# Spreading the attention denominators as high and low rows, and two reciprocals one expert unit earlier

## The reference

```python
q, k = relu(qkv[..., :8]), relu(qkv[..., 8:16]); v1 = concat([v, ones])
kv  = einsum('bgnd,bgne->bgde', k, v1)          # 32 heads of 8 channels
out = einsum('bgnd,bgde->bgne', q, kv)
out = out[..., :8] / (out[..., 8:] + EPS)       # numerators / denominators
x = x + batchnorm(conv1x1(out, w_proj))
t = (x - mean) / sqrt(var + 1e-5)               # norm over channels
probs = softmax(t @ router); keep the top 2 of 8
x = x + t + sum_e combine_e * (gelu(t @ w1[e] + b1[e]) @ w2[e] + b2[e])
```

## Time and profile before

| | us |
|---|---|
| median of three runs | 3474.5 |
| lowest and highest | 3469.59, 3474.97 |
| the profiled execution, its own time | 3470.55 |
| its span, first to last instruction | 3468.8 |
| TensorE busy | 3045.2 (88%) |
| VectorE busy | 1727.8 (50%) |
| ScalarE busy | 1512.8 (44%) |
| GpSimd busy | 853.9 (25%) |

### The profile page before, as it was taken

How to read it: one execution, slowest core, us unless ns; L and a number is a source line. 1 busy time by engine, 2 the same in 40 slices (tenths; PEclk the granted TensorE clock), 3 DMA queues, 4 the chain that set the end, 5 groups by cost and what they waited for, 6 DMA issues and landing times. The chain is left out here.

```text
span 3468.8 us, 66009 instructions
## 1 busy us (share of the span) xinstructions
PE 3045.2 (88%) x26432; PEld 1701.1 (49%) x26432; DVE 1727.8 (50%) x2317; ACT 1512.8 (44%) x2263; POOL 853.9 (25%) x694
## 2 busy tenths in 40 slices
PE   6766683899999975999998769999999999999989
PEld 1166321455555532566666234646454554646455
DVE  6724286577766440111111254656465555555575
ACT  4412351567677751111222344535454554545434
POOL 3500350344444421111110103121221213121322
PEclk7668675999999985999999789999999999999999
DMA  4611675123433324677777344655645564646244
GB/s 178 237 25 24 217 282 205 67 109 146 155 146 150 150 116 130 186 214 213 208 212 243 113 155 149 208 168 175 205 166 196 164 213 141 234 146 226 100 149 161
DMA packets 233863, 579.59 MB, mean 167 GB/s; under 512 B 38444, under 2 KB 105260, under 8 KB 225068
## 3 DMA queue, kind: packets, MB, share of 16 engines
q1 hardware_dynamic: 233684, 577.26, 49.8%
HBM read 384.24 MB, written 192.94 MB: 166 GB/s over the span
## 5 line engine op out<-in xcount | busy, mean ns | idle before, releaser
L2137 DVE TENSOR_TENSOR d_hid_scaled<-d_hid_scaled,d_gate 128x512 f32<-128x512 f32 x512 | 403.0, 799 | 437.1 <-PE d_ps L1835 266.2
L1835 PE MATMUL d_ps<-d_hid_scaled,d_w 128*128 128x512 f32 x1024 | 525.6, 595 | 4.3 <-DVE d_hid_scaled L2137 4.3
L1533 PE MATMUL c_ps<-c_pad,c_weight 32*32 32x512 f32 x13824 | 474.8, 601 | 26.1 <-ACT c_pad L1485 18.6
L2004 ACT ACTIVATE d_hid_scaled<-d_ps,d_b 128x512 f32<-128x512 f32 x512 | 349.7, 687 | 329.1 <-PE d_ps L1823 322.3
L1533 PEld LDWEIGHTS c_ps<-c_pad,c_weight 32*32 32x32 f32 x13824 | 287.0, 103 | 213.7 <-issue 129.4
L1821 PE MATMUL d_ps<-d_tnh,d_w1h 128*128 128x512 f32 x512 | 318.7, 623 | 19.8 <-ACT d_hid_scaled L2004 19.1
L1164 PE MATMUL b_ps<-b_hid,b_w2s 128*128 128x512 f32 x512 | 260.5, 593 | 0.0
L2089 POOL CAST d_tnh<-d_TN 128x512 fp32r<-128x512 f32 x64 | 47.3, 739 | 857.9 <-PE d_ps L1823 820.6
L1594 DVE COPY c_pad<-c_P 128x1024 f32<-128x1024 f32 x48 | 33.4, 696 | 414.5 <-PE c_ps L1533 379.2
L1485 ACT ACTIVATE c_pad<-c_P 128x1024 f32<-128x1024 f32 x48 | 51.8, 1079 | 392.2 <-PE c_ps L1533 372.0
L1835 PEld LDWEIGHTS d_ps<-d_hid_scaled,d_w 128*128 128x128 f32 x1024 | 194.4, 190 | 51.9 <-DVE d_hid_scaled L2137 5.7
(11 more groups left out here) (259 smaller groups left out, 5671.2 us busy)
## 6 DMA issues: line engine op xcount, KB each, us to landing
d_gate<-scratch_gates SPq DMA_DIRECT2D x256, 512.0 KB, 4.6
scratch_qkv<-b_qkv SPq DMA_DIRECT2D x64, 768.0 KB, 3.5
c_P<-scratch_qkv SPq DMA_DIRECT2D x192, 256.0 KB, 4.7
scratch_agg<-c_out SPq DMA_DIRECT2D x192, 256.0 KB, 4.9
d_buf<-scratch_qkv SPq DMA_DIRECT2D x96, 512.0 KB, 4.1
d_buf<-scratch_agg SPq DMA_DIRECT2D x96, 512.0 KB, 4.1
p_X<-in_x SPq DMA_DIRECT2D x8, 2048.0 KB, 8.4
scratch_s<-p_X SPq DMA_DIRECT2D x8, 2048.0 KB, 6.4
```

Of the source, the lines that this page charges most:

```text
L1533: end = nc.tensor.matmul(ps[on(i), k * QUADS + h, :].rearrange("p (b r w) -> p b r w", b=2, w=HB), weight[k][on(q), 2 * r + x, on(h)], pad ...
L1835: nc.tensor.matmul(moe_bank(n // E), w2[:, e, :], scaled[n % 3][:, :], start=False, stop=(e == E - 1)).then_inc(moe_pe, 1)
L2004: nc.scalar.activation(hid[n % 3][:, :], hid_bank(n), ACT.Gelu, bias=b1[:, n % E:n % E + 1]).then_inc(hid_done, 1)
L2137: nc.vector.tensor_tensor(scaled[n % 3][:, :], hid[n % 3][:, :], gate[k][:, n % 2 * CH:(n % 2 + 1) * CH], ALU.mult).then_inc(scaled_done, 1)
```

## The change

Four edits. (1) The reciprocals are split: VectorE copies them to a buffer of the single-pass type (`rech`) and subtracts that from the full value (`recl`), both 128x512, once for each image and head set; `cast` then multiplies `sel`, now of the single-pass type too, with `rech` and then `recl`, two products each, into the same banks. The buffers of s = 0 are those of the norm (`norm.high[0]`, `norm.parts[0]`). (2) There are two `den` buffers, the second being `fix[1]`, reciprocals are taken in place, and the second addition stands ahead of the second half of the first reciprocal. (3) `DEN` goes from 2 to 1 and (4) `INVERT` from 36 to 35. At the stage's start VectorE also converts `sel` once (128x256).

```diff
-        den, rec = sb("den", [128, CH]), two("rec", [128, CH])
-        rows = den
         fix = two("fix", [128, CH])
+        den = [sb("den", [128, CH]), fix[1]]
+        rows = den[0]
+        rech1, recl1 = sb("rech1", [128, CH], F32R), sb("recl1", [128, CH], F32R)
...
+        rech, recl = [norm.high[0], rech1], [norm.parts[0], recl1]
...
-        DEN, NUM, CAST, PROJECT, MEANS, CENTRE = 2, 4, 6, 9, 25, 28
-        INVERT, SCALE, LOGITS, TURN_LOGITS, EXP, KEYS, RELU = 36, 40, 43, 46, 49, 47, 58
+        DEN, NUM, CAST, PROJECT, MEANS, CENTRE = 1, 4, 6, 9, 25, 28
+        INVERT, SCALE, LOGITS, TURN_LOGITS, EXP, KEYS, RELU = 35, 40, 43, 46, 49, 47, 58
...
                     if p == 0:
-                        pe.wait_ge(rec_done, (b * 2 + s + 1) * 2)
+                        pe.wait_ge(rec_done, (b * 2 + s + 1) * 4)
...
-                    for r in range(2):
-                        c = 2 * p + r
-                        nc.tensor.matmul(bank(6 + r), sel[on(c % 4), c // 4, :], rec[s][on(c % 4), :], start=True, stop=True).then_inc(cast_pe, 1)
+                    for half in range(2):
+                        values = (rech, recl)[half][s]
+                        for r in range(2):
+                            c = 2 * p + r
+                            last = nc.tensor.matmul(bank(6 + r), sel[on(c % 4), c // 4, :], values[on(c % 4), :],
+                                                    start=(half == 0), stop=(half == 1))
+                    last.then_inc(cast_pe, 2)
...
-                    if b:
-                        dve.wait_ge(cast_pe, b * 4 * PAIRS)
                     half = slice(h * CH // 2, (h + 1) * CH // 2)
-                    nc.vector.reciprocal(rec[s][:, half], den[:, half]).then_inc(rec_done, 1)
-                    dve.wait_ge(rec_done, (b * 2 + s) * 2 + h + 1)
+                    nc.vector.reciprocal(den[s][:, half], den[s][:, half]).then_inc(rec_done, 1)
+                    dve.wait_ge(rec_done, (b * 2 + s) * 4 + h + 1)
+
+                def split_reciprocal(b, s):
+                    if b:
+                        dve.wait_ge(cast_pe, b * 4 * PAIRS)
+                    nc.vector.tensor_copy(rech[s][:, :], den[s][:, :]).then_inc(rec_done, 1)
+                    dve.wait_ge(rec_done, (b * 2 + s) * 4 + 3)
+                    nc.vector.tensor_tensor(recl[s][:, :], den[s][:, :], rech[s][:, :].bitcast(F32), ALU.subtract).then_inc(rec_done, 1)
+                    dve.wait_ge(rec_done, (b * 2 + s) * 4 + 4)
...
                     if i == DEN + 2:
+                        denominator(b, 1)
                         reciprocal(b, 0, 1)
-                        denominator(b, 1)
+                        split_reciprocal(b, 0)
                     if i == DEN + 3 or i == DEN + 4:
                         reciprocal(b, 1, i - DEN - 3)
+                    if i == DEN + 4:
+                        split_reciprocal(b, 1)
```

More of the change, by code:

```diff
@@ L1636, in phase_attention @@
         X, TN, ATT = sb("X", [128, 2 * HW]), sb("TN", [128, RING * CH]), sb("ATT", [128, HW])
-        w1_32, b2_32, b2_low = X[:, 0:E * 128], X[:, 2048:2176], X[:, 2176:2304]
+        w1_32, b2_32, b2_low, sel32 = X[:, 0:E * 128], X[:, 2048:2176], X[:, 2176:2304], X[:, 2304:2560]
         tables, back32, tile_consts = tile_tables(nc, ctx, "d_")
         ident = sb("ident", [128, 128])
-        heads, head_of, sel = sb("heads", [128, W]), sb("head_of", [128, HEADS]), sb("sel", [128, 2, 128])
+        heads, head_of, sel = sb("heads", [128, W]), sb("head_of", [128, HEADS]), sb("sel", [128, 2, 128], F32R)
         wp, bn, bnv = sb("wp", [128, 4, 2, 128]), sb("bn", [128, 4]), sb("bnv", [128, 4])
@@ L1678, in phase_attention @@
             ("tnh_done", "tnl_done", "xt_done", "up_pe", "hid_done", "scaled_done", "moe_pe", "fin_done")]
-        consts = tile_consts + [(heads[:, :], "heads"), (head_of[:, :], "head_of"), (sel[:, :, :], "head_rows"),
+        consts = tile_consts + [(heads[:, :], "heads"), (head_of[:, :], "head_of"), (sel32, "head_rows"),
                                 (wp[:, :, :, :], "wp"), (bn[:, :], "bn"), (wr[:, :], "wr1"), (before[:, :], "before"), (w1_32, "m1"),
@@ L2116, in _ @@
                 setup(nc.vector.tensor_copy(wide(tables[1]), wide(back32)))
+                setup(nc.vector.tensor_copy(wide(sel), sel32))
                 setup(nc.vector.tensor_copy(wide(w1h), w1_32))
@@ L2156, in denominator @@
                     dve.wait_ge(den_pe, b * 2 + s + 1)
-                    nc.vector.tensor_scalar(den[:, :], bank(5 + s), eps_a[:, :], None, ALU.add).then_inc(den_done, 1)
+                    nc.vector.tensor_scalar(den[s][:, :], bank(5 + s), eps_a[:, :], None, ALU.add).then_inc(den_done, 1)
                     dve.wait_ge(den_done, b * 2 + s + 1)
                 def reciprocal(b, s, h):
+                    half = slice(h * CH // 2, (h + 1) * CH // 2)
+                    nc.vector.reciprocal(den[s][:, half], den[s][:, half]).then_inc(rec_done, 1)
+                    dve.wait_ge(rec_done, (b * 2 + s) * 4 + h + 1)
+                def split_reciprocal(b, s):
                     if b:
                         dve.wait_ge(cast_pe, b * 4 * PAIRS)
-                    half = slice(h * CH // 2, (h + 1) * CH // 2)
-                    nc.vector.reciprocal(rec[s][:, half], den[:, half]).then_inc(rec_done, 1)
-                    dve.wait_ge(rec_done, (b * 2 + s) * 2 + h + 1)
+                    nc.vector.tensor_copy(rech[s][:, :], den[s][:, :]).then_inc(rec_done, 1)
+                    dve.wait_ge(rec_done, (b * 2 + s) * 4 + 3)
+                    nc.vector.tensor_tensor(recl[s][:, :], den[s][:, :], rech[s][:, :].bitcast(F32), ALU.subtract).then_inc(rec_done, 1)
+                    dve.wait_ge(rec_done, (b * 2 + s) * 4 + 4)
                 def weighted(b, p, s):
```

## The result

In the comparison on one chip the changed kernel took 3457.99 us in the median of 5 runs (3455.38 to 3462.02), the kernel before 3474.50 (3469.59 to 3480.68): ratio 0.9962, 95% interval 0.9945 to 0.9979, that is 7 to 19 us faster. The forecast was 3456.0, range 3438 to 3469. It also came into the last stage 4.0 us later (first denominators of image 0 at 1921.64 us, before at 1917.65). Of what the change adds, only the conversion of `sel` lies ahead of that, 0.29 us; in the traces of all runs this point lies between 1915.5 and 1926.9 us. From it to the end the changed kernel took 1538.6 us, the kernel before 1551.1: 12.5 us won in the stage that the change touches.

A forecast was written before the change was run, and what follows sets the result against it. TensorE was taken to bound the last stage, the other engines mostly waiting for it. Terms 17.2 + 2.8 - 4.9 - 5 + 5.6 - 0.3 = 15.4 us off 3470.55 gave 3455.1, stated as 3456; range 3438 to 3469.

The forecast's parts named there:

- Part 1: Late casts, images 1 to 7: each takes 0.65 us, not 1.06; 42 x 0.41 = 17.2 us won (7.6 to 26).
- Rival (b): Cast: its second pair costs as much as the first, 9.7 us less won, 3466 us; chance 0.2.
- Part 2: Denominators: the 2.30 us wait moves to the second cast and grows to 3.7; 2.8 us won (-6 to 10).
- Part 3: Norm's reciprocal: gelu of unit 37 is delayed, unit 40 starts about 0.7 us later; 4.9 us lost (0 to 8).
- Part 4: Clock: 7 or 8 falls at 14 longer waits, 1.5 us each; 5 us lost (-6 to 15).
- rival (c): Clock at second cast and unit 39: a fall of 3 us after every wait, kernel slower, 3486 us; chance 0.06.
- Part 5: Image 0, no experts beside it: earlier second addition and shorter casts win 5.6 us (3 to 7); sel's conversion loses 0.3.

The follow-up runs named there:

- e4: The changed kernel with NUM, CAST and PROJECT each two expert units later: 3448.86 us, 0.9927 of the kernel before.
- e7: The changed kernel with NUM, CAST, PROJECT two units later, MEANS one later, and the norm's parts behind the gelu of unit 37: 3424.05 us, 0.9863.
- e12: e7 with GpSimd's preparing of the next tokens four units later in units 8 and 40 only, and behind residual sums in its order: 3406.87 us, 0.9818.
- e5: The changed kernel with the norm's high and low parts one unit later in ScalarE's order, behind the gelu of unit 37: 3440.74 us, 0.9911.
- e8: The changed kernel with 14 useless products of constants ahead of both waits of each second cast: 3439.36 us, 0.9909.
- e9: The kernel before with NUM, CAST and PROJECT two units later and nothing else of the change: 3459.56 us, 0.9966.

## Why the prediction was right, step by step

The time was right, 2 us off, and so was the order of events. That it came so close is in part luck. In the last stage 12.5 us were won in the profiled executions where 15.4 were forecast: 6.1 in image 0 (forecast 5.6) and 6.4 behind it (forecast 10.1). The medians lie 16.5 us apart, and the interval for that difference is 7 to 19 us. Per image two sizes were off: the norm cost half of what was forecast and the clock twice as much, which left half of the forecast gain. In images 2 to 6, positive is won:

| part | forecast | measured | from |
|---|---|---|---|
| late casts, 6 x 0.41 | 2.46 | 2.4 | 0.66 for 1.06 at full clock |
| denominators and second `cast` | 0.4 | 0.2 | the rest of 187.01 - 184.82 |
| norm | -0.7 | -0.37 | 8.57 for 8.20 |
| clock | -0.7 | -1.5 | 2.9 each time, before 1.45 in the mean |
| sum | 1.4 | 0.7 | 188.46 - 187.75 |

**Part 1** held to 0.01 us. **Rival (b)** is false, and the rule of the Trainium skill ("TensorE: Matmul & The Clock Gate", Part 3, "The mechanism") that a weight load overlaps running products only where the row group differs does not hold for these rows: the second pair sits in the row groups of the first, its loads run from 2823.72, while the first pair's products run from 2823.61 to 2824.11, and from pair to pair it is 0.33 us, not 0.44.

**Part 2**: the step that the wait "moves to the second `cast`, and grows to 3.7 us" held (3.24), and so did GpSimd's meeting with the second split, 0.9 us of 1.2. The Trainium skill ("GPSIMD Engine Reference", "1. Specifications") lists the buffer interfaces as shared with VectorE, with contention for VectorE instructions that have two inputs there; the rows agree, 1.63 us beside GpSimd and 0.69 without. That the length of VectorE's row made the wait is shown in two steps: two units of room took it from 3.24 to 0.65 (e4), and moving GpSimd's work off the row, which made the row 1.0 us shorter, took it from 0.64 to nothing (e7 and e12).

**Part 3**: the order of events held, the failing term is "a unit is 1.7 to 1.8, so unit 40 starts at 2553.3", 7.2 us after the first half reciprocal. In the trace `up` of unit 39 comes at 5.26 us (forecast 5.5), since both halves end within 3.36, and unit 40 only 1.27 behind it, at 6.53; before it was 6.45. At `to_all` 0.37 us is lost. No fall came behind this wait. In e5 the order on ScalarE proved to be what makes this wait, as the step said.

**Part 4** had the number of falls right and failed in their price. "I take 7 or 8 falls: 3.5 x 1.5 = 5 us": at the fourteen waits there were seven, one in each of images 1 to 7 behind the wait at the second `cast`, none at the norm. But in images 2 to 7 the clock was down for the whole 6.2 us and not for a part of them, and each of these cost 2.9 us (e8). That is the size of rival (c), 3 us, which I had put aside because "the falls of before all ended within the step of 4.4 us". It came in six waits of fourteen only. With that price at all of them it would have cost 14 x 2.9 - 6 = 35 us against some 22 won elsewhere, and the kernel would have been slower than before; for the waits at the norm that price is not measured (where a fall came there, in e4 and e8, it cost 1.7).

**Part 5**: image 0, from its denominators to the turned gates, won 6.1 us (the lag of 4.0 us at its start became a lead of 2.1 at 2049.4), forecast 5.6. The conversion of `sel`, 0.29 us, lies ahead of it and is as forecast.

What stays open: why the same wait of 3.2 us ended in a clock of 0.50 in images 2 to 7 of the changed kernel, 0.72 in its image 1, and 0.50, 0.72 or 1.00 in e5. The runs show what a fall costs, not when it comes.

## What to carry to other kernels

Where TensorE's work is shared out to fixed slots, look first for a wait of phase: two slots of room (e9) gave what a rewrite of the products gave. The rewrite, the room, the other order on ScalarE and two of a neighbour's places moved out of the way gave four times as much together (e12). Follow the engine that is late to the end of its row before counting a removed wait as won, and look for what a third engine does beside its two-input operations. Price a wait of TensorE with what stands behind it at half clock: here a wait of 3.2 us brought 2.9 us more behind it, in images 2 to 7.

## What the runs showed of the hardware

- Fourteen products that compute nothing, put into a wait of 3.2 us, made the kernel 18 us faster (3439 and 3458 us; 0.9909 and 0.9962 of the kernel before), as the granted clock behind it was 1.00 and not 0.50.
- A second pair of single-pass products (fp32r, 32x128 by 32x512), in the same row groups as the first and accumulating on it, added 0.22 us to a single pair's 0.44; the float32 pair of before took 1.06.
- VectorE's subtraction of 128x512 with both inputs in the core's buffers took 0.69 us, and 1.63 beside GpSimd's subtraction; two scalings took 2.36 where two take 1.3, and a copy 0.97 in e7 where it took 0.43 in e12.
- Waits of TensorE of 2.1 to 2.7 us were followed by a fall of the granted clock in some images and not in others (before: four of fourteen), and the same wait of 3.2 us by 0.50, 0.72 or 1.00 over the next 6.2 us.
